# A transformer layer on one core: when the first block's weight sums are taken, where the last block's projection and tail stand, and small VectorE steps in slots of their own

## The reference

```python
x = x + xattn(layernorm(x), ctx)   # softmax(q k^T / 16) v, + its input, times Wo
x = x + mixer(layernorm(x))        # below
x = x + ffn(layernorm(x))          # 256 -> 1024 -> 256

# mixer: 512 inner channels, 16 states, rank 64
h = conv3(x @ in_w.T + in_b);  u = silu(h)
delta_lr, Bm = split(u @ x_proj_w.T + x_proj_b)
delta = softplus(delta_lr @ dt_w.T + dt_b)
carry = exp(delta * A) * carry + delta * u * Bm      # over the 32 tokens, for 512 x 16 states
y = sum over states(carry) + u * D;   out = y @ out_w.T + out_b

# ffn: ternary weights (sign and one scale, clip(mean|w|)), activations rounded to 127 steps of the row's maximum
out = bitlinear(silu(bitlinear(x, w_gate)) * bitlinear(x, w_up), w_down)
```

## Time and profile before

| | us |
|---|---|
| median of 3 runs | 1105.43 (1104.5 to 1112.4) |
| the profiled execution, its own time | 1107.78 |
| its span in the trace | 1106.0 |

### The profile page before, as it was taken

The page is one execution under the profiler, slowest core; times in us unless marked ns, Lnnn a source line. Parts: engine busy times, 40 slices in busy tenths (PEclk is TensorE's granted clock), DMA queues, the critical chain, the costliest instruction groups (busy, mean ns, idle before and its releaser), DMA issues.

```text
span 1106.0 us, 12743 instructions
## 1 busy us (share of the span) xinstructions
PE 943.5 (85%) x4007; PEld 491.5 (44%) x4042; DVE 903.5 (82%) x1210; ACT 755.4 (68%) x1320; POOL 857.9 (78%) x617
## 2 busy tenths in 40 slices
PE   6765698899989998999999998999899999777755
PEld 4441344354545453544545454545355454432333
DVE  2312687889998999899998999899989998799935
ACT  1216566787598769877798759876887768655524
POOL 0532999797979988897979797988879797989700
PEclk9778799999999999999999999999999999889967
DMA  9633252414205440525233420544042302200000
GB/s 342 218 131 123 107 178 91 164 60 165 109 21 191 159 166 20 192 77 177 91 120 118 169 111 20 191 153 172 20 172 96 115 20 82 110 0 1 27 12 20
DMA packets 22059, 124.71 MB, mean 113 GB/s; under 512 B 3496, under 2 KB 4136, under 8 KB 9449
## 3 DMA queue, kind: packets, MB, share of 16 engines
q1 hardware_dynamic: 16376, 89.09, 22.1%
q10 hardware_dynamic: 5616, 34.81, 8.2%
HBM read 115.23 MB, written 8.65 MB: 112 GB/s over the span
## 4 chain that ended last, share of the span: by engine, by line
PE 32%; ACT 22%; DVE 21%; POOL 10%; issue 9%; DMA 3%; SPq 1%; ACTq 0%; DVEq 0%; POOLq 0%
PE bank L977 19%; DVE state L853 10%; PE acc L977 10%; ACT decay L641 6%; POOL state L576 5%; DVE sg L902 2%; POOL rstd L539 2%; DVE hid L911 2%; DMA brep<-b_scratch 2%; POOL w L607 2%; ACT u L732 2%; ACT soft L627 2%; DVE hm L915 2%; ACT L740 2%; PE bank L1095 2%
## 5 line engine op out<-in xcount | busy, mean ns | idle before, releaser
L853 DVE TENSOR_TENSOR_SCAN state<-decay,state 128x512 f32<-128x512 f32 (+1 forms) x352 | 589.7, 1696 | 64.7 <-ACT decay L641 48.2
L576 POOL TENSOR_TENSOR state<-w,brep 128x512 f32<-128x512 f32 (+1 forms) x352 | 612.4, 1765 | 24.2 <-PE acc L977 24.0
L977 PE MATMUL acc<-state,ident 128*128 128x512 f32 x832 | 406.6, 608 | 12.9 <-DVE state L853 8.8
L641 ACT ACTIVATE decay<-delta,neg_a 128x496 f32<-128x496 f32 x512 | 327.3, 669 | 75.6 <-DVE state L853 68.9
L977 PEld LDWEIGHTS acc<-state,ident 128*128 128x128 f32 x832 | 148.0, 193 | 166.2 <-issue 110.3
L584 POOL TENSOR_TENSOR state<-state 128x512 f32<-128x512 f32 x96 | 122.2, 1273 | 61.5 <-DVE state L853 61.5
L668 ACT ACTIVATE sg<-bank,ag 128x512 f32<-128x512 f32 x64 | 43.6, 682 | 62.1 <-PE bank L977 61.4
L977 PE MATMUL bank<-xn_t,in_w 128*128 128x512 f32 x128 | 63.6, 632 | 7.6 <-DVE u L969 5.6
L607 POOL TENSOR_TENSOR w<-delta,u 128x512 f32<-128x512 f32 x32 | 39.9, 1266 | 36.2 <-ACT delta L764 36.2
L977 PE MATMUL bank<-out_w,u 128*128 128x256 f32 x256 | 57.4, 382 | 6.7 <-DVE u L844 6.7
L977 PE MATMUL bank<-u,xp_w 128*81 128x512 f32 x64 | 41.1, 803 | 19.2 <-ACT u L740 19.2
(11 more groups left out here) (137 smaller groups left out, 1306.8 us busy)
## 6 DMA issues: line engine op xcount, KB each, us to landing
keys<-in_keys_t SPq DMA_DIRECT2D x32, 1028.0 KB, 4.8
keys<-in_keys_n SPq DMA_DIRECT2D x32, 1024.0 KB
brep<-b_scratch ACTq DMA_DIRECT2D x32, 1024.0 KB, 6.8
x_scratch<-x_in SPq DMA_DIRECT2D x8, 512.0 KB, 2.6
res<-x_scratch SPq DMA_DIRECT2D x8, 512.0 KB, 3.2
out<-res SPq DMA_DIRECT2D x8, 512.0 KB, 8.6
x_in<-in_x SPq DMA_DIRECT2D x7, 512.0 KB, 5.4
brep<-in_w_gateT SPq DMA_DIRECT2D x1, 1024.0 KB, 13.4
```

The source lines that it names most:

```text
L576: nc.gpsimd.tensor_tensor(state[state_buffer(odd, g)][:, 0:count, :], w[:, m, :].unsqueeze(1).to_broadcast((P, count, TOK)), brep[:, n:n + ...
L641: last = nc.scalar.activation(decay[:, to + i, :, 1:LEN], d, ACT.Exp, scale=neg_a[:, m, n + i:n + i + 1])
L853: nc.vector.tensor_tensor_scan(flat, decay[:, of:of + count, :, :].rearrange("p c q l -> p (c q l)"), flat, 0.0, ALU.mult, ALU.add).then_i ...
L977: return nc.tensor.matmul(o, l, r, start=first, stop=last)
```

## The change

1. The tables `POST`, `PRE`, `LAST` and `PREPARE` are written anew; most parts move by 0 to 4 steps of the 88.
2. `s_max` becomes `s_max`, `s_neg`, `s_bias`; `h_max` becomes `h_max`, `h_floor`, `h_scale`; `conv` becomes `tap0`, `tap2`. Each is a part with steps of its own, between which other parts and scans can stand.
3. In phase 8 PE gets four parts `out_ahead` at steps 70, 72, 74 and 76: each does the products of channel tiles 0 to 2 of block 7 for one token tile, into banks D and E. In phase 9 `out_proj` then does only channel tile 3, and `x2` reads D and E. `up` number 2, the first that writes D and E, waits for `x2` there.
4. ACT does one exponential of 4 columns before the first phase.

The core of the diff, with the table entries that matter:

```diff
 POST (before -> after)
-("h_max", [22, 32, 55, 73])            -("scale_h", [29, 34, 69, 75])   -("h_evac", [32, 36, 71, 77])
+("h_max", [19, 31, 54, 72])            +("scale_h", [25, 33, 70, 75])   +("h_evac", [30, 35, 74, 80])
+("h_floor", [21, 31, 60, 72])
+("h_scale", [22, 32, 67, 73])
 PRE
-("s_max", [14, 16, 28, 33])            -("exp", [13, 19, 29, 35])       -("z_turn", [24, 32, 40, 45])
+("s_max", [13, 16, 25, 33])            +("exp", [13, 19, 29, 37])       +("z_turn", [23, 30, 36, 44])
+("s_neg", [14, 17, 26, 34])
+("s_bias", [14, 20, 28, 36])
-("p_turn", [16, 25, 33, 41])           -("attend", [22, 28, 35, 44])    -("p_evac", [19, 28, 34, 41])
+("p_turn", [12, 26, 31, 39])           +("attend", [13, 26, 34, 42])    +("p_evac", [17, 27, 33, 40])
-("conv", [59, 61, 66, 66])             -("dt", [73, 82, 85, 86])        -("softplus", [81, 87])
+("tap0", [59, 62, 65, 65])             +("dt", [73, 78, 85, 87])        +("softplus", [84, 87])
+("tap2", [60, 62, 65, 66])
-("b_load", [78, 78, 81, 84])           -("stats1", [1])                 -("add2", [58])
+("b_load", [77, 79, 79, 87])           +("stats1", [0])                 +("add2", [63])
 LAST
-("h_max", [33, 52, 76, 86])            -("hidden", [16, 27, 37, 40, 71, 72, 78, 80])
+("h_max", [35, 42, 64, 73])            +("hidden", [26, 33, 39, 42, 56, 63, 66, 73])
+("h_floor", [39, 44, 67, 85])          +("h_scale", [39, 49, 70, 86])
-("finish", [68, 73, 87, 87])           -("gate", [16, 27, 32, 38, 70, 72, 78, 79])
+("finish", [49, 62, 87, 87])           +("gate", [18, 27, 27, 39, 49, 56, 63, 69])
 PREPARE
-("abs_sum", [6, 11, 14, 14])  -("mixer_weights", [6])   -("vo", [9])  -("vo_evac", [14])  -("total", [12])
+("abs_sum", [8, 22, 24, 39])  +("mixer_weights", [29])  +("vo", [7])  +("vo_evac", [38])  +("total", [35])
-("scales", [23])  -("quantise", [44, 50, 52, 59])
+("scales", [42])  +("quantise", [29, 48, 54, 57])
+TAIL = [("out_ahead", [70, 72, 74, 76])]
...
+            nc.scalar.activation(esum[:, 0:1], eps4[:, 0:1], ACT.Exp).then_inc(prep_a, 1)
...
+                def out_tile(m, i, odd):
+                    return mm(bank[:, (D, E)[i // 2], (i % 2) * DIM:(i % 2 + 1) * DIM],
+                              u[odd][:, m, i * P:(i + 1) * P], out_w[:, m, :], m == 0 and i % 2 == 0,
+                              m == TILES - 1 and i % 2 == 1)
...
+                            else:
+                                last = out_tile(TILES - 1, i, par)
                         last.then_inc(mixed, 1)
+                    elif part == "out_ahead":
+                        reach(pe, y_ready, b, TILES - 1)
+                        reach(pe, delta_ready, b, TILES)
+                        for m in range(TILES - 1):
+                            out_tile(m, g, odd)
...
                         elif g == 2:
-                            reach(pe, delta_ready, b, TILES)
+                            reach(pe, x2_ready, b, 2)
```

More of the change, by code:

```diff
@@ L55 @@
-    ("hidden", [16, 19, 25, 29, 44, 49, 66, 69]),
-    ("out_proj", [2, 2]),
-    ("rstd3", [6]),
+    ("x_turn", [7]),
+    ("rstd3", [3]),
+    ("gate", [15, 18, 21, 23, 42, 45, 59, 69]),
+    ("scale_h", [25, 33, 70, 75]),
+    ("xn3", [9]),
+    ("h_max", [19, 31, 54, 72]),
+    ("h_turn", [27, 33, 72, 78]),
+    ("h_scale", [22, 32, 67, 73]),
+    ("h_evac", [30, 35, 74, 80]),
+    ("x2", [4, 5]),
+    ("stats3", [5]),
+    ("y_last", [0]),
+    ("up", [9, 12, 17, 23, 37, 43, 48, 67]),
+    ("x_max", [9]),
@@ L68 @@
-    ("exp", [13, 19, 29, 35]),
-    ("stats1", [1]),
-    ("p_turn", [16, 25, 33, 41]),
-    ("turn2", [55]),
-    ("add1", [47]),
-    ("times_u", [82, 82, 87, 87]),
-    ("silu", [62, 67, 67, 68]),
-    ("evac1", [5]),
-    ("z_turn", [24, 32, 40, 45]),
-    ("u_evac", [58, 61, 63, 63]),
-    ("dt", [73, 82, 85, 86]),
-    ("x1", [49, 51]),
-    ("stats2", [52]),
-    ("softplus", [81, 87]),
-    ("attn_out", [46, 46]),
-    ("query", [4]),
-    ("s_max", [14, 16, 28, 33]),
-    ("b_load", [78, 78, 81, 84]),
@@ L86 @@
-    ("rstd1", [0]),
-    ("attend", [22, 28, 35, 44]),
-    ("xn2", [53]),
-    ("score", [9, 12, 23, 29]),
-    ("q_evac", [8]),
-    ("xn1", [4]),
-    ("z_evac", [22, 32, 37, 43]),
-    ("p_last", [18, 25, 32, 39]),
-    ("rstd2", [53]),
-    ("add2", [58]),
-    ("evac2", [55]),
+    ("xn1", [5]),
+    ("query", [6]),
+    ("exp", [13, 19, 29, 37]),
+    ("softplus", [84, 87]),
+    ("x_dbl", [72]),
+    ("turn2", [55]),
+    ("p_last", [14, 23, 31, 37]),
+    ("xn2", [54]),
+    ("p_turn", [12, 26, 31, 39]),
@@ new lines @@
+    ("tap0", [59, 62, 65, 65]),
+    ("p_sum", [16, 26, 33, 42]),
+    ("b_load", [77, 79, 79, 87]),
+    ("stats1", [0]),
+    ("attend", [13, 26, 34, 42]),
+    ("rstd2", [52]),
+    ("evac1", [7]),
+    ("evac2", [56]),
+    ("z_evac", [20, 29, 35, 44]),
+    ("tap2", [60, 62, 65, 66]),
+    ("zt_evac", [26, 31, 38, 45]),
+    ("attn_out", [45, 46]),
+    ("rstd1", [0]),
+    ("q_evac", [9]),
+    ("x1", [49, 51]),
+    ("s_neg", [14, 17, 26, 34]),
+    ("s_max", [13, 16, 25, 33]),
+    ("p_evac", [17, 27, 33, 40]),
@@ L106 @@
[L106 to L121 removed]
+    ("x_evac", [17]),
@@ new lines @@
+    ("finish", [49, 62, 87, 87]),
+    ("h_floor", [39, 44, 67, 85]),
+    ("h_turn", [44, 62, 85, 86]),
+    ("stats3", [9]),
+    ("scale_h", [34, 35, 63, 70]),
+    ("x_turn", [23]),
+    ("xn3", [0]),
+    ("up", [26, 27, 27, 34, 49, 65, 75, 75]),
+    ("down", [46, 69, 87, 87]),
+    ("h_scale", [39, 49, 70, 86]),
+    ("y_last", [2]),
+    ("out_proj", [1, 8]),
+    ("h_evac", [34, 49, 75, 87]),
+    ("scale_x", [6]),
+    ("tanh", [18, 33, 33, 33, 39, 62, 62, 62]),
+    ("x2", [3, 7]),
+    ("hidden", [26, 33, 39, 42, 56, 63, 66, 73]),
@@ L134 @@
+    ("vo_evac", [38]),
+    ("mixer_weights", [29]),
+    ("abs_sum", [8, 22, 24, 39]),
 ]
@@ L428, in slots @@
                     yield "chunk", j, at - SLOTS, par
+                for stage, part, g in TAIL_AGENDA[step] if scan and not pre else ():
+                    yield part, j - 1, g, 1 - par
                 for stage, part, g in (AGENDA if pre or scan else LAST_AGENDA)[step]:
```

129 lines of the change are left out of this document (61 added, 68 removed).

## The result

The changed kernel takes 1088.45 us (median of 4 runs, 1087.98 to 1090.81) against 1106.49 beside it on the same chip. The ratio is 0.9855, with a 95% interval of 0.9819 to 0.9891; it is taken over the fast executions alone, so it is not the quotient of the two medians. The forecast was 1081, range 1066 to 1098: faster, inside the range, 7.5 us above the forecast. The profiled execution has a span of 1086.4 us and an own time of 1088.2.

What follows compares the result with a forecast made beforehand. No engine full throughout; in six full phases DVE and PE nearly full, DVE setting pace. Start -2.6, phase 1 -1.5, full phases -15.0, phase 8 -0.6, projection -5.4, end +0.3: -24.8 us, median 1081, range 1066 to 1098.

Steps and rivals of the forecast that it cites:

- The projection early: Between last `y_last` and `x2`: three quarters of the last projection moves into PE's free time in phase 8, -5.4 us.
- Small steps apart: DVE in full phases: parting dependent neighbours saves 0.12 to 0.18 us each, 1.3 us a phase, bounds 0 and 1.7.
- Rival 2: DVE: dependences cost nothing, so parting small steps gives nothing; median 1089.6, chance 0.15.
- Moved parts: Full phases: new order removes parts of four stalls, 1.2 us net a phase, bounds 2.9 gained and 2.9 lost.
- Rival 4: ACT: `exp` waits for a later `s_bias` and decays queue behind it, 6.8 us a phase; median about 1126, chance 0.05.
- The four waits named: DVE stalls of 1.72, 1.22, 0.66 and 0.42 us a full phase, of which 2.9 of 4.0 us can go.
- rival 1: Full phases give nothing: each removed stall is replaced, PE being as full as DVE; median 1097.7, chance 0.17.
- The sign I had named for it: DVE's waits for decays in full phases should add up to about 1.5 us a phase instead of 3.6.
- The order at the end: Phase 9: the new order ends 0.3 us later than before, bounds -0.8 and +2.4.
- Reciprocal 1 behind `finish` 0: Phase 9: ACT's scaling of tile 1, and `tanh` 4 behind it, come 1.2 us or more later.
- The start: Before the first scan: weight sums later, so queries are evacuated and scores start earlier; -2.6 us, bounds 0 and -5.2.
- The extra exponential: Start, ACT: moves the 1.28 us table load into idle time; counted as nothing since PE is busy until 14.49.

Runs made afterwards that it cites:

- experiment 2: Kernel before with only the projection of three channel tiles moved into phase 8; 1102.69 us, ratio 1.001.
- experiment 9: Kernel before with twelve extra products on PE between the two halves of `vo` in the start; 1104.5 us, ratio 0.9982.
- Experiments 3 and 4: Changed kernel with small DVE steps together again: 3 with all new tables, 1099.96 us; 4 with old `POST` and `PRE`, 1105.01 us.
- experiment 7: Changed kernel with small steps apart but all other parts at the old steps of `POST` and `PRE`; 1118.04 us, ratio 1.014.
- experiment 1: Changed kernel with the last phase's order of before put back; 1083.4 us, ratio 0.9827.
- experiment 11: Changed kernel, new end order, with extra products on PE all through phase 9; 1086.69 us, ratio 0.9822.
- experiment 6: Changed kernel with evacuation 2 and down 2 ahead of the last tile's turn, in the last phase alone; 1090.01 us, ratio 0.9878.
- experiment 10: Changed kernel with the last phase's DVE steps in the order of before, PE, ACT and POOL in the new; 1088.08 us, ratio 0.9814.
- experiments 11 and 12: Changed kernel with extra products on PE all through phase 9: 11 with the new end order, 1086.69 us; 12 with the old, 1079.93 us.

## Why the prediction was right or wrong, point by point

**The projection early: right for the turn, wrong in that phase 8 pays nothing.** The turn: -5.2 against -5.4. `x2` followed the last `y_last` by 2.63 us and not 2.0; on the DVE timeline it was waiting for another transfer:

```profile
1032.30 1.29 DVE L892 TENSOR_TENSOR res<-bank,res 128x512 f32<-128x512 f32 x2 [1.87 <-DMA res<-x_scratch]
```

What I wrote as free in phase 8 costs 2.0 to 4.2 us in the old order, by way of ACT (experiment 2); I had 1.34 at most, by way of PE's sums. The whole phase still came out 1.8 us shorter, 1.2 better than predicted; its waits, the last `y_last` included, fell from 9.0 to 8.1 us. But the kernel of experiment 9 has the phase 8 of before and takes 103.13, less than after, so the 1.8 is not shown to be the change's.

**Small steps apart: right, and by the steps given.** I took 1.3 us of each full phase, 7.8 over six, with a bound of 1.7 (10.2). Rival 2, dependences that cost nothing, is refuted by two comparisons of the rest that change only the parting: 9.6 us (new tables, 13 places) and 11.6 (old tables, 15 places), or 0.12 and 0.13 us for each place. So nearly all of it counted, not three quarters. From before to after the rest fell by 5.7, since the moved parts gave 3.7 back. The Trainium skill's sentence in "VectorE: DVE Perf Modes", section "The DRAIN you can't avoid", that a semaphore between chained operations adds nothing, doesn't give the right price for these short steps: a dependent neighbour costs 0.12 us and more against an independent one.

What I left out is that parting has a second effect through ACT, and that its sign depends on the tables: +26.4 us of waits in the old ones, -3.0 in the new. The 3.0 are not clear of what equal kernels differ by, the 26.4 are. "Rival 4" with a chance of 0.05 is no curiosity but what the change would have been without the moved parts. My argument against it, that the decay which DVE needs next stands before `exp`, holds for the new tables alone.

**Moved parts: the step that failed.** I had "1.2 us as net", 7.2 over six phases. The four waits named went nearly as said: decays 26.9 to 12.7 us, or 2.4 us a phase, where I had 0.6 + 1.2 and 0.66 as the parts that can go. But 7.6 us of new waits for PE's sums, 3.1 for `finish`, 2.6 for the taps and 1.6 for `gate` came, and 2.5 us was left. This is rival 1 for this term, whose reason (PE as full as DVE) was also the right one: parts that come earlier on PE push the sums. I had walked along the old waits and not along the new order of PE. The sign I had named for it, decay waits of about 1.5 us a phase, came to 2.1. Experiments 3 and 4 put it more sharply: without the parting the moved parts cost 4.3 us, 3.7 of them in the rest, where I had counted a gain of 7.2. The two terms don't simply add: parting alone is +14.8 us, moving alone +4.3, both together -8.2. What the moved parts are good for is to make room for the later results of the parted steps: ACT's waits for those results are 29.1 us in experiment 7 and 0.6 in after. My sum had no such term.

**The order at the end: the second step that failed.** +5.5 instead of +0.3, outside my bound of +2.4. I counted it as a gain that "the two last turns and downs follow each other on PE". The last steps of after, on all engines:

```profile
1075.92 1.97 PE L1137 MATMUL bank<-ident,hid 128*128 128x128 f32 x8 [0.81 <-ACT hid L690]
1077.68 1.91 PE L1004 MATMUL bank<-down_q,hq_t 128*128 128x256 bf16 x8
1079.63 1.27 ACT L696 ACTIVATE hq_t<-bank,unmagic 128x512 bf16<-128x512 f32 x2 [2.61 <-PE bank L1004]
1080.95 1.89 PE L1004 MATMUL bank<-down_q,hq_t 128*128 128x256 bf16 x8 [1.36 <-ACT hq_t L696]
1082.87 0.48 DVE L948 SCALAR_TENSOR_TENSOR res<-bank,beta,res 128x256 f32<-128x256 f32 x1 [2.76 <-PE bank L1004]
```

and with the old end order (experiment 1):

```profile
1077.68 1.09 PE L1137 MATMUL bank<-ident,hid 128*128 128x128 f32 x8 [0.60 <-ACT hid L690]
1078.44 1.27 ACT L696 ACTIVATE hq_t<-bank,unmagic 128x512 bf16<-128x512 f32 x2 [0.81 <-PE bank L1137]
1079.76 1.05 PE L1004 MATMUL bank<-down_q,hq_t 128*128 128x256 bf16 x8 [0.98 <-ACT hq_t L696]
1080.84 0.48 DVE L948 SCALAR_TENSOR_TENSOR res<-bank,beta,res 128x256 f32<-128x256 f32 x1 [3.24 <-PE bank L1004]
```

There is one buffer `hq_t` for the turned and rounded hidden values. The evacuation of the last tile must wait until down 2 has read it (2.61 us of waiting, ended by PE at 1079.6), and down 2 stands behind the last turn. From the last turn's start to the finish after takes 7.0 us, the old order 3.2, and four runs part this: order new and clock full 5.2 (experiment 11), order mended and clock half 4.6 (experiment 6), both good 3.2, both bad 7.0. So 2.0 to 2.4 us are the order and 1.4 to 1.8 the clock, as far as one execution each can say; the 5.2 hold extra products too. Before had 4.6: old order, half clock. That is 2.4 of the 5.5 us. The other 3.2 lie in front of the last turn, which starts 30.0 us after the first gate product instead of 26.8. Reciprocal 1 behind `finish` 0, the step that I priced at "1.2 us or more", is not shown to be it. With the reciprocal back at its maximum the end is 1.9 us shorter in experiments 3 and 4 (35.08 and 34.92), but there down 0 and turn 1 ran at full clock (1.05 and 1.04 us); in experiment 10, where they took 1.89 and 1.85, it is 0.3 shorter. How those 3.2 us divide between the order and the clock of down 0 and turn 1 stays open.

**The start: right in its first step, short by a clock.** The start of after, on PE and ACT:

```profile
23.77 0.69 ACT L714 ACTIVATE soft<-bank,q_bias 128x512 f32<-128x512 f32 x1 [1.98 <-PE bank L1004]
...
28.25 2.71 PE L1004 MATMUL bank<-o_w,brep 128*128 128x256 f32 x8
...
31.76 1.08 PE L1004 MATMUL bank<-keys,soft 128*32 128x257 f32 x16
...
52.09 1.13 PE L1004 MATMUL bank<-vo_w,soft 128*128 128x256 f32 x4 [0.47 <-ACT soft L741]
```

The queries are evacuated at 24.46 (predicted 24.3), `vo` stands where I put it, and score 1 starts at 31.76 (predicted 32.8, before 36.92). That is -5.2 instead of -4.1; the row of biases in front of score 0 took 1.95 us instead of 3.41. From there to the output projection after needs 20.3 us and before 23.5: -3.1, at a granted clock of 0.94 and 1.00 against 0.56 and 0.96. Another -1.2 up to x_proj (93.45 to 83.96), then +0.5 as given back. I worked out the times of the steps with those of before, which ran at half clock from 29.7 to 43 us.

That the clock belongs to the change is not shown. Seven kernels with exactly the start code of after had their first scan at 97.3 to 106.4 us, mean 100.9; two with that of before at 108.9 and 106.1. The means differ by 6.6 us, which is the better size of this term, though with two kernels on the one side, and the two groups touching, it is good to a few microseconds only; 2 to 3 us of the measured 9.0 are then the luck of one execution. In the same way the full phases of those seven took 712.2 to 718.6 us, mean 714.7, and of four with the old ones 721.1 to 721.9: -7.0 rather than -8.2, and here the groups lie apart.

The extra exponential does what was said, nothing: the first normalisation starts at 10.94 us with no table load in front of it, and PE's first turn is at 14.58 us, against 14.35 before.

**The sum.** -9.0 - 1.0 - 8.2 - 1.8 - 5.2 + 5.5 = -19.7, and 0.1 from roundings and the last DMA. That the forecast came near is in part luck: 6.4 us too little in the start and 1.2 in phase 8 stood against 6.8 too much in the full phases and 5.2 too little cost at the end. Of the six terms the turn was right in size and in mechanism, and the parting in mechanism; the range held the result although two of its steps had failed.

## What to carry to other kernels

Split a phase into waits (the list of waits, summed from mark to mark) and the rest before judging a reordering: gaps of dependences and stalls changed with opposite signs in experiment 7, and only the two numbers apart said so. Take care that both ends of the list are the marks themselves: one wait too many at an end was 1.6 of 8.2 us here. Moving small dependent steps apart saved 0.12 to 0.13 us a place on DVE, but what reads the last of them on another engine gets it later, so it must be moved too: the same parting was worth -12.6 us over six phases in one order and +14.8 in another. Where a late part "follows directly" on one engine, check each single buffer between the two: an evacuation that must wait for the reader of the same buffer turns an overlap into a chain.

## What the runs showed of the hardware

- TensorE's granted clock differs between executions at the same place of the same code: 1.00 and 0.50 from 42 to 56 us in two kernels with equal starts. The first scan differs by 6.5 us between them; the one at 0.50 had also waited 2.88 us for a transfer just before.
- Extra products did raise the clock where they stood (0.78 against 0.56 in the start; 0.89 and 1.00 over the last 30 us of experiments 11 and 12, where after has 0.61), but after the start's block PE was granted 0.61 from 42 to 56 us where before had 0.96, and no use of them made the path clearly shorter.
- On DVE an instruction that depends on nothing started 0.08 to 0.09 us before the end of the one ahead of it, behind a small step as well as behind a reduction (experiment 7); a dependent one started 0.04 and 0.10 us behind that end.
